# Splitting the last round of an expert router in two, with idle-time products on TensorE

## The reference

```
z      = layernorm(x)                          # after the cross-attention and its output projection
scores = z @ gate_w.T + gate_b + bias          # 8 scores of a row
top_scores, top_idx = top_k(scores, 2)
gates  = softmax(top_scores)
h      = silu(einsum(z, w1[e]) + b1[e])        # 512 -> 352, for every expert e
y      = einsum(h, w2[e]) + b2[e]              # 352 -> 512
x      = x + sum over the two experts of gate * y
```

## Time and profile before

| | us |
|---|---|
| median of 3 runs | 660.88 |
| lowest and highest | 657.59, 663.14 |
| the profiled execution: its own time | 661.93 |
| the profiled execution: span from first to last instruction | 660.0 |
| mean granted TensorE clock over the span | 0.913 |

### The profile page before, as it was taken

How to read it: one execution, slowest core, us unless ns; L and a number is a source line. 1 busy time by engine, 2 the same in 40 slices (tenths; PEclk the granted TensorE clock), 3 DMA queues, 4 the chain that set the end, 5 groups by cost and what they waited for, 6 DMA issues and landing times.

```text
span 660.0 us, 10081 instructions
## 1 busy us (share of the span) xinstructions
PE 553.8 (84%) x3342; PEld 341.3 (52%) x3342; DVE 360.5 (55%) x989; ACT 267.8 (41%) x611; POOL 194.6 (29%) x237
## 2 busy tenths in 40 slices
PE   4889695999999999869998998998840699999980
PEld 2454343545555555436766776676630455555540
DVE  4453777667676685267778677777353222222210
ACT  1027771412222232158988677775310122222220
POOL 1010303123123321143446455542705021221220
PEclk9969986999999999979999899896755799999996
DMA  8994770322231200130533123312513245445425
GB/s 324 298 419 119 253 235 0 128 94 70 93 129 51 93 1 0 61 111 13 189 99 111 54 58 111 100 57 83 159 45 103 66 82 96 77 86 97 75 39 131
DMA packets 32663, 72.74 MB, mean 110 GB/s; under 512 B 4042, under 2 KB 19434, under 8 KB 30562
## 3 DMA queue, kind: packets, MB, share of 16 engines
q1 hardware_dynamic: 28198, 63.48, 29.6%
q0 software_dynamic: 4416, 8.63, 8.1%
HBM read 46.40 MB, written 27.33 MB: 112 GB/s over the span
## 4 chain that ended last, share of the span: by engine, by line
PE 59%; DVE 19%; DMA 7%; issue 5%; POOL 4%; ACT 4%; SPq 1%; POOLq 0%; DVEq 0%; ACTq 0%
PE ps L818 9%; PE ps L1123 8%; PE ps L1109 8%; PE ps L812 7%; PE ps L893 4%; DMA w1s<-in_win 4%; PE ps L952 4%; PE ps L876 4%; PE ps L1055 3%; DVE sN L1449 2%; PE ps L944 2%; PE ps L965 2%; ACT hTe L781 1%; POOL g L497 1%; DVE VS L1190 1%
## 5 line engine op out<-in xcount | busy, mean ns | idle before, releaser
L812 PE MATMUL ps<-CT,wkS 128*128 128x364 f32 x224 | 77.8, 501 | 9.3 <-DMA wkS<-in_wk 9.3
L728 ACT ACTIVATE pE<-sN,nmx 100x361 f32<-100x361 f32 x128 | 77.7, 607 | 6.2 <-DVE nmx L1449 6.1
L818 PE MATMUL ps<-wvS,CT 128*121 128x512 f32 x168 | 77.0, 607 | 0.0
L1449 DVE CUSTOM_DVE_ANT_0 sN<-ps,maskS 100x361 f32<-100x361 f32 x128 | 62.0, 531 | 11.3 <-PE ps L944 5.8
L952 PE MATMUL ps<-ident,pE 100*121 100x100 f32 x384 | 63.2, 294 | 1.3 <-ACT pT L719 1.1
L606 POOL DMA_INDIRECT sums_out<-yb,backI x20 | 31.1, 1554 | 109.7 <-ACT yb L791 105.7
L952 PEld LDWEIGHTS ps<-ident,pE 100*121 100x121 f32 x384 | 51.9, 200 | 21.5 <-issue 20.2
L812 PEld LDWEIGHTS ps<-CT,wkS 128*128 128x128 f32 x224 | 44.7, 204 | 35.6 <-issue 14.8
L1123 PE MATMUL ps<-VS,hTe 118*128 x120 | 56.7, 609 | 5.5 <-ACT hTe L781 5.5
L719 ACT COPY pT<-ps 121x300 f32<-121x300 f32 x128 | 51.8, 404 | 22.5 <-PE ps L952 22.3
L1574 DVE TENSOR_TENSOR hb<-ps,b1B 128x352 f32<-128x352 f32 x20 | 10.5, 524 | 88.2 <-PE ps L1109 88.2
(11 more groups left out here) (248 smaller groups left out, 958.5 us busy)
## 6 DMA issues: line engine op xcount, KB each, us to landing
slots_in<-zeros SPq DMA_DIRECT2D x8, 1848.0 KB, 8.9
VS<-in_w SPq DMA_DIRECT2D x6, 1024.0 KB, 30.1
CT<-in_ew SPq DMA_DIRECT2D x8, 704.0 KB
VS<-in_ew SPq DMA_DIRECT2D x8, 672.0 KB
xin<-slots_in SPq DMA_DIRECT2D x20, 264.0 KB, 2.8
CT<-in_ctxT SPq DMA_DIRECT2D x7, 728.0 KB, 11.9
ahead<-in_w SPq DMA_DIRECT2D x2, 1024.0 KB, 34.0
summB<-summary_rows SPq DMA_DIRECT2D x8, 200.0 KB
```

The lines of the kernel that those rows point to most:

```text
L728: act.activation(pE[0:S, q, 0:T], sN[0:S, q, 0:T], ACT.Exp, scale=-1.0, bias=nmx[0:S, h_:h_ + 1], accum_out=sums[0:S, j, h_:h_ + 1]).then_ ...
L812: mm = pe.matmul(ps[:, at, 0:TP], wkS[:, k, m * P:(m + 1) * P], ctx(b)[:, k * TP:(k + 1) * TP], start=(k == 0), stop=(k == KC - 1))
L818: mm = pe.matmul(ps[0:TC, at, :], ctx(b)[:, k * TP + c * TC:k * TP + (c + 1) * TC], wvS[:, k, :], start=(k == 0), stop=(k == KC - 1))
L1449: dve.tensor_tensor_reduce(out=sN[0:S, q, 0:T], in0=ps[0:S, q, 0:T], in1=maskS[0:S, j, 0:T], scale=-1.0, scalar=3.4e38, op0=ALU.add, op1=A ...
```

## The change

The second round is cut in two: batches 4 and 5 are routed in a round of their own (`THEN = 6`), and 6 and 7 in a third, with PSUM bank 5. The places of the last round and the counts are separate functions now. TensorE issues products that nobody reads (`fill`, 112 columns, and `hold_clock`, 512 columns) at four places.

```diff
-FIRST = 4
+FIRST, THEN = 4, 6
+FILL, FILL_LONG = 6, 10
...
             rstd_z(B - 1)
-            send(FIRST, B, 2)
+            send(FIRST, THEN, 2)
+            send(THEN, B, 3)
...
             turned_z(B - 2, 1)
+            second_share(FIRST, THEN, 2)
             turned_z(B - 1, 2)
-            second_share(FIRST, B, 2)
+            second_share(THEN, B, 3)
...
-            def last_places():
-
-                pe.wait_ge(sem("hot"), 2)
-                pe.matmul(ps[0:S, 3, 0:(B - FIRST) * E], before[0:S, 0:S], both[:, FIRST * E:B * E], start=True, stop=False)
-                pe.matmul(ps[0:S, 3, 0:(B - FIRST) * E], ones[0:S, 0:S],
-                          total[0:S, 0:B - FIRST, :].rearrange("p b e -> p (b e)"), start=False, stop=True)\
+            def more_places(lo, hi, bank, rounds):
+
+                n, at = (hi - lo) * E, lo - FIRST
+                pe.wait_ge(sem("hot"), rounds)
+                pe.matmul(ps[0:S, bank, 0:n], before[0:S, 0:S], both[:, lo * E:hi * E], start=True, stop=False)
+                pe.matmul(ps[0:S, bank, 0:n], ones[0:S, 0:S],
+                          total[0:S, at:at + hi - lo, :].rearrange("p b e -> p (b e)"), start=False, stop=True)\
                   .then_inc(sem("places"), 1)
+
+            def last_counts():
                 pe.matmul(ps[:, 4, 0:E], ones[0:S, :], total[0:S, B - FIRST, :], start=True, stop=True)\
                   .then_inc(sem("counts"), 1)
+
+            def fill(products):
+                for i in range(products):
+                    pe.matmul(ps[:, 6, KC * S:512], ident[:, :], ident[:, 0:512 - KC * S], start=True, stop=True)
...
             logits(B - 3, 0)
+            fill(FILL)
             pe.wait_ge(sem("oQb"), after(B))
             turn_rows(oQb, "oq_t", B - 1)
             turn_z(B - 2, 1)
             out_rows(B - 1)
             logits(B - 2, 1)
+            fill(FILL)
+            more_places(FIRST, THEN, 3, 2)
             turn_z(B - 1, 2)
             logits(B - 1, 2)
-            last_places()
+            fill(FILL)
+            more_places(THEN, B, 5, 3)
+            last_counts()
             pe.wait_ge(sem("experts_in"), 48 * E)
+            hold_clock(FILL_LONG)
...
-            def last_totals():
-
-                for b in range(FIRST, B):
+            def more_totals(lo, hi):
+
+                for b in range(lo, hi):
...
             norm_z(B - 2)
             take_logits(B - 3, 0)
+            pick_best(0, FIRST, THEN)
+            pick_second(FIRST, THEN)
             finish5(B - 1)
             x_out(B - 1)
             stats_z(B - 1)
+            more_totals(FIRST, THEN)
             norm_z(B - 1)
             take_logits(B - 2, 1)
+            make_shares(FIRST, THEN, 2)
+            make_slots(FIRST, THEN, 3, 2)
             take_logits(B - 1, 2)
-            pick_best(0, FIRST, B)
-            pick_second(FIRST, B)
-            last_totals()
-            make_shares(FIRST, B, 2)
-            make_slots(FIRST, B, 3, 2)
+            pick_best(0, THEN, B)
+            pick_second(THEN, B)
+            dve.wait_ge(sem("hot"), 2)
+            more_totals(THEN, B)
+            make_shares(THEN, B, 3)
+            make_slots(THEN, B, 5, 3)
```

More of the change, by code:

```diff
@@ L1409, in first_total @@
                    .then_inc(sem("hot"), 1)
-            def last_totals():
-                for b in range(FIRST, B):
+            def more_totals(lo, hi):
+                for b in range(lo, hi):
                     i = b - FIRST
                     ins = dve.tensor_tensor(total[0:S, i + 1], total[0:S, i], hot[0:S, 2, b], ALU.add)
-                    if b < B - 1:
+                    if b < hi - 1:
                         ch(ins)
```

## The result

The changed kernel took 654.54 us in the median, against 662.04 for the kernel before in the same comparison: a ratio of 0.9892 (95% interval 0.9864 to 0.9921). The profiled execution took 654.45 with a span of 652.2, so against the one of before the span is 7.8 shorter. One of the seven executions behind the median took 1401.33 us and isn't in the ratio; without it the median is 654.50. The forecast was 654.6, as 660.88 less 6.3 us. A later comparison of the same two kernels gave 0.9891.

A forecast was written before the change was run, and what follows sets the result against it. No engine is full in the 27 us handover from stage B to the experts; each step waits for the last. -5.28 - 0.6 + 0.5 = -5.4, with clock -0.9: -6.3 from 660.88 gives 654.6; range 653 to 656.5, 8 in 10 650.8 to 658.6.

The forecast's parts named there:

- Four sends leave the chain, -5.28: GpSimd's sends: with four issued earlier, the last starts 4.10 behind the first instead of 9.38, saving 5.28 us.
- VectorE's shorter list, -0.6: VectorE's last round: summing two batches instead of four saves 0.38, narrower operations about 0.2; together -0.6 us.
- The picks ahead of `finish5`, +0.2: VectorE: thirteen operations for batches 4 and 5 before batch 7's `finish5`, mostly covered by a projection wait; delay 0 to 0.3.
- TensorE's list, with the former +0.5, at half clock +0.9: TensorE before batch 7's scores: second fill and places delay them 0.9 at half clock, 0.1 at full; middle +0.5, including +0.2.
- at half clock the two end at 488.2: TensorE: second fill (3.1) and round two's places (0.87) after 484.24 end at 488.2, before batch 7's `z` is turned.
- From the last send to the first turn, nothing expected: Landing of the last send, load of block 0, TensorE's first turn: the prediction named no change here.
- the 5 to 6 that the prediction had set as its own sign: Block 0's first turn on TensorE: the prediction is wrong if it isn't 5 to 6 us earlier.
- The clock, -0.9: Block 0: the hold ends between 505 and 508, the level probably falls once more around block 0's start; -0.9 us.
- 3.3: First blocks on TensorE: upper end of the saving in us if block 0 runs at full clock; the lower end is 0.
- The level lost at 479.9 in spite of the fill: TensorE's 3.5 us wait, now holding 1.7 us of products: whether that keeps the clock was left open, middle taken.
- A lock held by the sends: Rival: early sends hold VectorE's picks through the SBUF port pair, up to 0.9 us each, +3.6, giving 658.2; chance 0.07.

The follow-up runs named there:

- e1: The changed kernel with its split round but none of the products without use (no fill, no long hold); 0.9908 of the kernel before, median 655.13 us.
- e7: The changed kernel with `THEN = 5`: batch 4 alone in round two, so two sends early and six late; 0.9961 of the kernel before.
- e6: The changed kernel with twelve products instead of six in the second fill; 0.9970 of the kernel before.
- e8: The changed kernel with sixteen long hold products instead of ten; 0.9925 of the kernel before.
- e4: The changed kernel with twelve long hold products instead of ten, and one more behind block 0's turn; 0.9848 of the kernel before.

## Why the prediction was right, step by step

The mechanism was right: the split takes four sends out of the chain, and that is most of the gain (6.1 us in e1). That 654.6 and 654.54 agree to 0.1 us is luck. The forecast subtracted 6.3 from a median of 660.88; in the comparison the kernel before stood at 662.04, and the gain was larger, 7.2 us by the ratio and 7.8 between the profiled executions. The steps for these two:

- *Four sends leave the chain, -5.28.* Right: 4.10 from first to last instead of 9.38, and e7 shows the two steps of 1.32 each, from the other side.
- *VectorE's shorter list, -0.6.* Right: from batch 7's scores to the slot numbers 5.79 (490.40 to 496.19) against 6.41, -0.62; the two sums took 0.36.
- *The picks ahead of `finish5`, +0.2.* It started at 483.24 instead of 483.16: +0.08. The cover held, as said.
- *TensorE's list, with the former +0.5, at half clock +0.9.* The clock was at half, the premise of the worse end, and yet the cost was +0.01: scores at 490.40. This is the term that was mis-sized. Here the step "at half clock the two end at 488.2" was wrong in size. I added 3.1 for the fill, twice the 1.55 of three products, and 0.87 for the places, from a row before which TensorE had been idle. In the trace the fill began at 484.07 and took 2.88, and the places began inside its last 0.2 us and were out at 487.48. `z` was ready at 487.30 and was turned from 487.35, so the cover was used up to less than 0.1 us. That nothing was paid is luck: in e7 the same fill began 0.11 later against `z`, and the turning came 0.68 behind the start of `z` instead of 0.60; in e6 the fill was 2.56 longer and the turning 2.54 later.
- *From the last send to the first turn, nothing expected.* 6.96 instead of 7.14, -0.18. Without e8, whose hold was in the way, it varied from 6.96 to 7.68. The two DMAs in it, the landing and the load of block 0, hold the difference; why they differ I didn't find.
- The first turn thus came 6.10 earlier, not 5.4, which is just outside the 5 to 6 that the prediction had set as its own sign.
- *The clock, -0.9.* The forecast was that the hold ends between 505 and 508, that the level falls once around the start of block 0, and that a short dip leaves half of 3.3. The hold ended at 506.45, the level fell at 510.6 for 3.4 us, and blocks 0 and 1 took 1.18 less. Of this the hold's own share is 0.5 to 1.2, as the runs without it show, so the -0.9 lies within what they show, and no more can be said. e4 gives the upper end of the term: 8.34 from the first turn to the end of the second group, so 2.7 in all, where 3.3 was written. Its groups take 2.63 at full clock, not 2.4, so the first gains 2.3 and the second nothing; I had taken the even pattern of the later blocks for them.
- *The level lost at 479.9 in spite of the fill:* I had taken the middle between lost and kept. It was lost, also with 2.17 us of wait.
- *A lock held by the sends:* not seen. The picks beside the sends took 0.17 to 0.18, one a step of 0.21 (491.21 beside the send of 490.97). Here the trace doesn't agree with the rule on the port pair in the Trainium skill ("SBUF — State Buffer", "Who interferes with whom") if a send counts as a GpSimd instruction that reads SBUF.

The sum for the profiled executions: -6.10 to the first turn, -1.18 in the two groups, and -0.5 from there to the end (134.2 against 134.7), which no step named. The last term isn't the change's as far as the runs show: it was between 133.9 and 134.9 in all of them.

## What to carry to other kernels

A step that issues many DMAs one after the other costs its count times its step behind the last input; cutting the inputs into rounds hides the early rounds where they lie under other work, as four sends did here. Their part of the gain, 5.28 us, could be read from the profile of before; the terms around it were off by up to half a microsecond. Products that keep TensorE's clock up paid here only close to the work they were meant for: ten of them with a wait of 7.4 or 5.1 us behind gave nothing, ten with 1.7 to 2.0 gave 0.5 to 1.2 us, and twelve with one behind the turn gave all 2.7. Before trusting a cover that looks full, double what lies in it and look.

## What I had not expected of the hardware

- In TensorE's timeline a group starts 0.1 to 0.2 us before the end that is shown for the one ahead of it (486.75 against 486.95), and six small products at half clock took 2.88, not twice the 1.55 of three.
- The level was still up after a wait of 1.70 us behind 5.9 us of unbroken products at full clock, and was lost at the end of one of 2.17 us and inside two of 2.8 us, with less ahead of them. No run separates the length of the wait from what stood before it.
- How early stage B ended differed by 12 us between the traces (`oQb` from 471.2 to 483.65). Of two traces of the same changed kernel one had it 5.4 us earlier (474.12 against 479.47) and its batch 7 `z` only 2.6 earlier (484.12 against 486.75): the other 2.7 went into the wait behind round one's sends.
